# A six-layer attention stack in fp32, twice: the value projection folded into the output projection, and attention applied to the shifted tile itself

## What is computed

```python
def attn_layer(x, Wqkv, qs, ksc, Wo):            # x: [b, n, 128], already token-shifted
    q, k, v = jnp.split(x @ Wqkv, 3, -1)         # 128 -> 1024 each: 16 heads of 64
    q = l2norm(sh(q)) * qs;  k = l2norm(sh(k)) * ksc
    q, k = rotary(q) * scale, rotary(k) / scale
    out = local_attention(q, k, sh(v))           # windows of 32 tokens, each sees itself and the window before
    return out.transpose(0, 2, 1, 3).reshape(b, n, INNER) @ Wo      # 1024 -> 128

for i in range(DEPTH):                           # DEPTH = 6, and the whole stack runs twice
    x = attn_layer(shift_tokens(x), Wqkv[i], q_scale[i], k_scale[i], Wo[i]) + x
    x = ffn_layer(shift_tokens(x), ...) + x      # layer norm, 128 -> 2 x 341, gelu gate, 341 -> 128
```

## Time and profile before

| what | before |
|---|---|
| median of three runs | 3374.68 us |
| the profiled execution: its own time | 3380.69 us |
| its span | 3378.9 us |
| mean granted TensorE clock | 0.994 |
| PE busy | 97% of the span |
| DVE, ACT, POOL busy | 82%, 72%, 66% |
| DMA | 170.06 MB, mean 50 GB/s |

### The profile page before, as it was taken

One profiled execution on the slowest core, in us unless ns is written; L12 is line 12 of the kernel. 1 busy time (PEld: TensorE's weight loads), 2 busy tenths in 40 slices (PEclk: granted clock), 3 DMA queues, 4 the chain that ended last, 5 costly groups with the idle time before them and its releaser, 6 DMA issues. The chain is left out here.

```text
span 3378.9 us, 150942 instructions
## 1 busy us (share of the span) xinstructions
PE 3288.9 (97%) x63515; PEld 2482.8 (73%) x63515; DVE 2758.7 (82%) x6952; ACT 2424.5 (72%) x3769; POOL 2227.0 (66%) x1454
## 2 busy tenths in 40 slices
PE   6999999999999999999999999999999999999998
PEld 3777777777777777777777777777777777777776
DVE  5788888888888888889998888888888888888885
ACT  2777777777777777777777777777777777777775
POOL 4666666666666666667888666666666666666663
PEclk7999999999999999999999999999999999999999
DMA  3111111111111111111111111111111111111111
GB/s 115 51 48 51 48 48 50 48 51 47 48 46 51 48 51 48 49 49 48 50 42 51 48 50 48 48 50 48 51 45 48 48 51 48 51 48 51 50 51 42
DMA packets 199180, 170.06 MB, mean 50 GB/s; under 512 B 139610, under 2 KB 172525, under 8 KB 198509
## 3 DMA queue, kind: packets, MB, share of 16 engines
q1 hardware_dynamic: 193901, 157.05, 17.1%
q10 hardware_dynamic: 4608, 3.34, 0.3%
HBM read 33.38 MB, written 1.05 MB: 10 GB/s over the span
## 5 line engine op out<-in xcount | busy, mean ns | idle before, releaser
L1112 POOL TENSOR_TENSOR rot<-rot,swp 128x1024 f32<-128x1024 f32 x384 | 907.4, 2363 | 140.0 <-DVE rot L901 140.0
L705 ACT ACTIVATE sq<-proj 128x512 f32<-128x512 f32 x768 | 437.7, 596 | 551.2 <-PE proj L503 540.0
L503 PE MATMUL proj<-wq,xsT 128*128 128x512 f32 x1536 | 772.4, 625 | 14.4 <-DVE rot L901 10.2
L1121 POOL TENSOR_TENSOR rot<-rot,rn 128x1024 f32<-128x1024 f32 x384 | 724.4, 1908 | 0.0
L1102 POOL TENSOR_TENSOR rt<-rt,half 128x1 f32<-128x1 f32 x192 | 105.3, 548 | 807.0 <-DVE rt L971 807.0
L895 DVE TENSOR_TENSOR swp<-proj,tab 128x512 f32<-128x512 f32 x768 | 522.6, 680 | 17.0 <-ACT sq L705 13.6
L901 DVE TENSOR_TENSOR rot<-proj,tab 128x512 f32<-128x512 f32 x768 | 519.7, 677 | 1.5 <-PE tps L514 1.5
L514 PEld LDWEIGHTS tps<-idf,rot 128*128 128x128 f32 x3072 | 360.2, 141 | 207.3 <-issue 203.4
L1025 DVE SCALAR_TENSOR_TENSOR hT<-proj,b1c,fg 114x128 f32<-114x128 f32 (+1 forms) x576 | 166.7, 345 | 419.7 <-ACT fg L769 414.2
L1106 POOL TENSOR_TENSOR prob<-prob,rr 128x1024 f32<-128x1024 f32 x192 | 365.4, 1903 | 186.0 <-DVE rr L983 186.0
L540 PEld LDWEIGHTS sps<-kT,qT 64*32 64x32 f32 x24576 | 366.0, 106 | 134.8 <-issue 134.4
(11 more groups left out here) (111 smaller groups left out, 5743.0 us busy)
## 6 DMA issues: line engine op xcount, KB each, us to landing
vb<-va SPq DMA_DIRECT2D x192, 384.0 KB, 3.5
vb<-va SPq DMA_DIRECT2D x192, 128.0 KB, 3.4
wq<-in_L_ffn_Wqkv SPq DMA_DIRECT2D x95, 192.0 KB
xs<-Z SPq DMA_DIRECT2D x384, 32.0 KB
xs<-Z SPq DMA_DIRECT2D x384, 28.0 KB
xs<-Z SPq DMA_DIRECT2D x384, 3.8 KB
xs<-Z SPq DMA_DIRECT2D x384, 0.2 KB
wo<-in_L_ffn_Wo SPq DMA_DIRECT2D x94, 64.0 KB
```

What stands on the lines that cost most here:

```text
L503: mm(proj[:, c % 2, :], xsT[:, k.parity(L_QKV), :], wq2[:, bass.ds(w + c * 512, 512)], start=True, stop=True).then_inc(p_qkv[c], 1)
L705: fn(sq[:, c * 512:(c + 1) * 512], proj[:, c % 2, :], ACT.Square).then_inc(a_sq[c], 1)
L1112: g_.tensor_tensor(r, r, swp[:, g * INNER:(g + 1) * INNER], ALU.add).then_inc(g_add[g], 1)
L1121: g_.tensor_tensor(r, r, rn[:, g * HEADS:(g + 1) * HEADS].unsqueeze(2) .to_broadcast([P, HEADS, DH]), ALU.mult).then_inc(g_nm[g], 1)
```

## The change

The weights `Wv_h @ Wo_h` of a layer (128x128 for each of 16 heads) are made on the chip into `wvo`, in eight pieces of two heads, one piece every second step: one transpose (L518), then two matmuls of 64 rows (L438), and two small copies on ACT; the first layer's are made at once after step 2 (`FOLD`). `project` is left for q and k alone (L392); the value projections and their copies are gone. `attend` is called twice in a step, for the even and the odd windows g (L433): each call has two matmuls of 64 rows, a stationary tile of 64x128 (the shifted tile `xs`, or its copy one window later, `xr`) and 512 columns of `pT`. Both calls write both banks of `ops`, so ACT copies `ops` into `oT` after each (`attended`). `oT` now has 16 tiles of 128x128, and `Wo` is 16 matmuls of 128x128 by 128 (L536). `Wo` stands behind the transpose of the normalised tile, no longer ahead of the transposes of the probabilities (L493). On DVE, the addition of attention to `Z` comes after the last piece of the reciprocal square root, and `bn_stats` moved from the end of a step to a place between the rotations of halves 0 and 1 of the next. The window-shifted copy is made from `xs` (now a ring of 8) in 64 KB instead of 512 KB. Dead branches of `Step` and a flag table are removed, too.

```diff
-                if k.on(L_AV):
-                    k.wait(a_pT, L_AV)
...
+            def attend(k, g):
+                u = k.tile(L_AV)
+                for t in range(2):
+                    rows = slice(t * DH, (t + 1) * DH)
+                    x = xr[rows, u % 2, :] if g == 0 else xs[rows, u % RING, :]
+                    last = mm(ops[:, t, :], x, pT[rows, :, g * 2 * WIN:(g + 1) * 2 * WIN], start=True, stop=True,
+                              skip_group_check=True)
+                last.then_inc(p_O[g], 1)
...
+            def fold(wvT, wo, out, rows):
+                return mm(out, wvT[rows, :], wo[rows, :], start=True, stop=True, skip_group_check=True)
...
                     k.wait(a_qT, L_S)
                     transpose_rot(1, p_kT)
-                if k.on(L_WO):
-                    weights(k, L_WO, d_wo, CHUNKS)
-                    k.wait(a_oT, L_WO)
-                    w = k.layer_parity(L_WO, PAIRS * P)
-                    for p in range(PAIRS):
-                        last = mm(ops[:, 0, 0:P], oT[:, p, :], wo[:, bass.ds(w + p * P, P)], start=(p == 0),
-                                  stop=(p == PAIRS - 1))
-                    last.then_inc(p_wo, 1)
+                if k.on(L_AV):
+                    k.wait(a_oT[0], L_AV)
+                    attend(k, 1)
...
-                if k.on(L_S):
-                    weights(k, L_S, d_wq, CHUNKS)
-                    k.wait(v_ab[3], L_QKV)
-                    values(k, 1)
+                if k.piece(0) is not None:
+                    n = k.piece(0)
+                    pe.wait_ge(d_wvo[n % 2], 32 * (n // 2 - PAIRS // 2 + 1))
+                    k.wait(a_kT, L_S)
+                    k.wait(a_pT, L_SM)
+                    tr(tps[:, 1, :], wv[:, n % 2, :], idf[:, :]).then_inc(p_wvT, 1)
                 if k.on(L_F):
                     k.wait(a_xn, L_F)
                     k.wait(a_kT, L_S)
                     k.wait(a_pT, L_SM)
+                    if k.piece(1) is not None:
+                        n = k.piece(1)
+                        pe.wait_ge(a_wvT, n - PAIRS + 1)
+                        for hp, to in ((0, 2), (1, 6)):
+                            last = fold(wvT, wo[:, n % 2, :], tps[:, to, :], halves2[hp])
+                        last.then_inc(p_wvo, 1)
                     tr(tps[:, 0, :], xn[:, :], idf[:, :]).then_inc(p_xnT, 1)
-                if k.on(L_S):
-                    k.wait(v_ab[2], L_QKV)
-                    values(k, 0)
+                if k.on(L_WO):
+                    if k.tile(L_WO) >= TILES:
+                        pe.wait_ge(a_wvo, k.tile(L_WO) // TILES * PAIRS)
+                    k.wait(a_oT[1], L_WO)
+                    for h in range(HEADS):
+                        last = mm(ops[:, 0, 0:P], oT[:, h, :], wvo[:, k.layer_parity(L_WO), h // 2, h % 2, :],
+                                  start=(h == 0), stop=(h == HEADS - 1))
+                    last.then_inc(p_wo, 1)
...
+            def attended(k, g):
+                if k.on(L_AV):
+                    k.wait(p_O[g], L_AV)
+                    k.wait(p_wo, L_WO + 1)
+                    o4 = oT[:, :, :].rearrange("p h (t g i) -> p t h g i", t=2, g=2)
+                    cp(o4[:, :, :, g, :], ops[:, :, :].rearrange("p t (h i) -> p t h i", i=WIN)).then_inc(a_oT[g], 1)
```

More of the change, by code:

```diff
@@ L48 @@
 FRONT = 6
[L49 to L51 removed]
+FOLD, PREPARE = 2, 3
+RING = 8
+PIECE = 12
 X_NEXT = 4
@@ L278, in layer_parity @@
[L278 to L285, removed]
-                    between(s)
[L288 to L316, removed]
+            def wait_pair(self, sms, lag, per):
+                u = min(self.s - lag, T - 1)
+                if u >= 0:
+                    self.eng.wait_ge(sms[u % 2], (u // 2 + 1) * per)
@@ new lines, in wait_mid, with piece, pipeline @@
+            def wait_mid(self, sm, lag):
+                t = min(self.s - lag - (N - TILES), TILES - 1)
+                if t >= 0:
+                    self.eng.wait_ge(sm, t + 1)
+            def piece(self, late):
+                n, odd = divmod(self.s + PIECE - late, 2)
+                return n if not odd and PAIRS <= n < LAYERS * PAIRS else None
+        def pipeline(eng, step, between=None, last=T + L_F2):
+            for s in range(last):
+                step(Step(eng, s))
+                if between is not None and s < FRONT:
+                    between(s)
@@ L757, in step @@
                     cp(xnT[:, :], tps[:, 0, :]).then_inc(a_xnT, 1)
-                if k.on(L_S):
-                    k.wait(p_O, L_S + 2)
-                    k.wait(d_vb, L_S + 1, per=32)
-                    values(k, 1)
-                    values(k, 0)
+                if k.piece(0) is not None:
+                    k.wait(p_xnT, L_F)
+                    n = k.piece(0) - PAIRS
+                    act.wait_ge(p_wvT, n + 1)
+                    if n:
+                        act.wait_ge(p_wvo, n)
+                    cp(wvT[:, :], tps[:, 1, :]).then_inc(a_wvT, 1)
                 if k.on(L_F):
@@ L961, in step @@
                 if k.on(L_F):
-                    k.wait(v_bn, L_F)
+                    k.wait(d_xs2, L_F, per=64)
+                    v.bn_stats(st[:, :], xs2[:, :]).then_inc(v_bn, 1)
                 if k.on(L_QKV):
@@ L1037, in step @@
                                     .to_broadcast([P, 2, PAIRS, 2 * WIN]), ALU.subtract).then_inc(v_sub, 1)
[L1038 to L1041 removed]
+                if k.on(L_F2) and k.tile(L_F2) >= T - TILES:
                     t = k.tile(L_F2) - (T - TILES)
@@ L1076, in _ @@
             dve.wait_ge(c_zero, 1)
-            pipeline(dve, step, between, end=OUT - 1)
+            pipeline(dve, step, between)
         @block.gpsimd
```

431 lines of the change are left out of this document (175 added, 256 removed).

## The result

The changed kernel takes 3798.47 us (median of four runs, 3796.91 to 3799.38) where the kernel before takes 3374.92: the ratio is 1.1247, 95% interval 1.1233 to 1.1260. It is slower by 424 us. Forecast were 3770 and a range of 3680 to 3850.

What follows compares the result with a forecast made beforehand. PE was taken as the bound, at 17.18 us per step; opened waits make it 19.2 (9.0 + 10.1, pauses 0.1). +386 over 191 steps, +7 folding, +2 drain give 3776 profiled, 3770 as median; range 3680 to 3850.

Steps and rivals of the forecast that it cites:

- S to Q: From the end of the scores (S) to the start of the probabilities' transposes (Q): 9.0 us instead of 9.35.
- the first wait: PE waits for POOL's normalisation before the transposes of the probabilities, partly already at the k projections: some 1.5 us per step.
- rival (b): Attention's t halves run one after the other, 0.86 us more in each call: 3846 us; chance 18%.
- rival (e): Edges of array tile changes cost a full drain, +0.3 or so beyond the wait at Q: near 3827; 5%.
- My 16.92: PE's work alone in a new step, in us, against 16.80 before, without waits.
- rival (a): No waits open and PE is the bound, step 16.92 us: faster, 3334 us; chance 5%.
- after Q: From the probabilities' transposes to the end of the next scores: 10.1 us instead of 7.45.
- 2.13: Time in us after Q when PE goes on, having waited 0.6 for ACT's copy of the transposed probabilities.
- The pauses: PE stops on "issue" inside the scores, outrunning instruction delivery: 0.38 us per step before, 0.1 taken for the new step.
- rival (c): Pauses inside the scores stay as they are, +0.28 us per step: 3823 us; chance 13%.
- its full 0.20: `bn_stats`, moved into DVE's chain ahead of POOL's normalisation, lengthens that chain by 0.20 us per step.
- Folding the first layer: After step 2 the first layer's weights are folded with nothing beside it: about +7 us.

Runs made afterwards that it cites:

- Experiment 1: Changed kernel with half of the columns of both attention calls left out (0.86 us less PE work per step): 3800.62 us.
- experiment 2: Changed kernel with 4 of the 16 `Wo` matmuls of a step left out: 3637.32 us.
- experiment 3: Kernel before, with only its 8 `Wo` matmuls, DVE's addition and `bn_stats` at the changed kernel's places: 3649.85 us.
- late_wo_in_four: Changed kernel with `Wo` one step later, in four parts of 4 matmuls, and two buffers for `oT`: 3427.1 us.
- experiment 5: Changed kernel with only `bn_stats` on DVE back at the end of the step before: 3788.03 us.
- before_wo_moved: The same run as experiment 3, kernel before with `Wo`, DVE's addition and `bn_stats` at the new places: 3649.85 us.

## Why the prediction was right, and where it was off

**The mechanism held.** S to Q was forecast at 9.0 and is 8.95 and 9.16 in turn; the chain over DVE and POOL is 8.90 long, and the rotation comes 5.45 after S against my 5.5. That ACT's copy of k ends last in every second step wasn't in the forecast. Experiment 1 shows the first wait by what removing work did not bring, experiment 2 that the second part is PE's own, experiment 3 that the new order alone opens the wait.

**The work of PE** came out in size: `Wo` takes 3.57 and 3.64 from start to start against 3.66. The two halves t of attention run side by side: a call takes 1.06 up to the next group in `late_wo_in_four`, and rival (b) asked for 1.8. I had 0.97. If they overlap wholly, the edge coming out of the 64-row mode is 0.20 (1.06 - 0.86) and not the 0.11 that the old attention showed. The Trainium skill, TensorEngine Tiling (Array Packing), section Tiling Modes, has it that every change of mode drains TensorE. The trace agrees that there is a price, and puts it at 0.1 going in and 0.2 coming out. In the changed kernel the waits for the rotation and at Q hid what the calls of attention pay, so rival (e) stayed false. My 16.92 for a step's work was too low all the same. I counted the 0.11 out of the old attention twice (its 2.00 to the next group holds it already, so 2.10 stood against my 2.14, and not 2.21). And in `late_wo_in_four`, where nothing hides the work, a step takes 16.92 without the pieces and 17.28 with them. The time of the changed kernel didn't hang on this sum, since its first part is bound by the chain; that of rival (a) did.

**The terms that were too small** lie after Q, where I had 10.1 and the steps show 10.45 and 10.05 in turn. PE went on 2.40 and 2.26 after Q instead of 2.13: with `pT` copied at 1507.33 (1506.32 + 1.01), the 64-row matmuls of the piece start at 1507.58, 0.25 later, where I had allowed 0.05 for waking up, and in the other kind of step a transpose starts there 0.15 later (1488.44, after a copy done at 1488.29). The matmuls of a piece take 0.43, as forecast. On the other side of the balance the pauses at the scores fell away altogether, where I had kept 0.1, so rival (c) was wrong, and this hid a part of the error. Together 9.06 + 10.25 = 19.31 against 19.2. The pauses had never been the whole 0.38 that I gave them: all 62 at the scores are 41.7 us, 0.22 per step.

**`bn_stats`** I counted with its full 0.20 in every step; experiment 5 gives back some 10 us, a quarter. The chain grew by 0.16 or 0.17 (8.73 before, 8.74 with `bn_stats` back, 8.90), and in every second step ACT's copy of k sets Q, behind the copy of the carry, which I hadn't followed into the forecast.

**The ends.** Folding the first layer was put at +7. The masks of the first and the third of the early steps (start, us):

```profile
42.21 1.03 PE L415 MATMUL sps<-mask,idb 128*128 128x512 bf16 x2 [3.55 <-DVE rn L805]
...
102.50 0.59 PE L415 MATMUL sps<-mask,idb 128*128 128x512 bf16 x2
```

are 60.3 apart where the same two steps before took 49.2, from 43.39 to 92.57. So +11, and the fold itself isn't what I missed: it takes 6.74, from 46.47 to 53.21. The scores on either side of it are slower, at the lower level of the clock. The two stretches of mask and scores now (granted clock third from the end), and the first of them before:

```profile
42.21:46.47 4.26, 4.26 (x131) 3.34 (x131) 0.00 (x0) 0.00 (x0) 4.26 (x4) 0.55 0.09 26
67.94:72.47 4.53, 4.53 (x131) 3.53 (x131) 0.00 (x0) 0.00 (x0) 4.53 (x4) 0.50 0.01 4
43.39:45.86 2.47, 2.47 (x132) 1.95 (x129) 0.00 (x0) 0.75 (x2) 2.47 (x3) 1.00 0.11 28
```

Before, the second stretch took 2.47 too, so this is 3.9 of the 11. The granted clock is at or near 1.2 GHz here, right behind idle PE (3.55 us ahead of the first, 2.04 ahead of the second), where it was 2.4. Ahead of the first scores the kernel before had its value projections, and they stood in the slow stretch instead (0.53 from 39.91 to 43.28).

My 28 us too few can then be added up from the masks. From the first mask to the last (42.21 to 3752.50, before 43.39 to 3343.64) the changed kernel takes 410 us more, where I had 393: 4 of these 17 are the opening, 13 the steps. 2.11 per step lie between the third mask and the last, less than the 2.15 of the stretch, since the last layer has no pieces and its steps lose only 1.9 (18.99 against 17.08). What lies ahead of the first mask and behind the last is 6 longer, where I had 2. The last 8 come from taking the median 6 below the profiled execution, when it lay 1.6 above.

## What to carry to other kernels

In a step where engines hand work round in a circle, ask of every block what it covers before moving or splitting it: `Wo` cost 1.9 us of work, and its old place also hid 1.5 us of someone else's latency. An engine at 97% isn't the only bound, since the chain beside it was 0.6 us short of PE's own time; when a block grows, let it work on the result of the step before and cut it to fit the waits. And fewer instructions and bytes are worth only what the trace shows to be waiting for them, here 0.22 us per step at the scores (41.7 / 191).

## What the runs showed of the hardware

Two fp32 matmuls of 64 rows x 128 columns with 512 moving columns, on the upper and the lower half of the array and into two banks, take 1.06 us together, the edge coming out included, where one full matmul of 512 columns takes 0.86. That they overlap at this shape, no row had shown before. The edge of the mode was dearer coming out (0.20) than the small matmuls of the old attention had let it seem (0.11). In the opening, where PE had idled for 3.55 and 2.04 us just before, the granted clock was 0.55 and 0.50, and the same mask and scores took 4.26 and 4.53 us instead of 2.47. And the pauses on "issue" in a dense stretch of small matmuls vanished without any fewer instructions, once PE waited 1.5 us in each step (`before_wo_moved`).
